# A recurrent stage rearranged: nine single instructions for the deviations, a mix 1024 columns wide, products and transposes in blocks

## The chip, the cores and the metric

One core of a Trainium2 chip runs the whole kernel. The metric is the time of one execution in microseconds (us); the median of three runs of the kernel before is 3341.35 us. The engines are PE (TensorE: matmuls, and transposes as matmuls with a unit matrix), PEld (its weight loads, which overlap with PE), DVE (VectorE), ACT (ScalarE), POOL (GpSimd) and SP (SyncE, which issues most DMAs). Each works through its own list of instructions in order. They meet at semaphores: counters that an instruction raises when it ends and that another engine's instruction waits for.

## The reference, cut to what matters

The program is a transformer over 128 graphs of 128 nodes with 128 channels, four stages that each add to x: graph attention, a mixture of experts, a second graph attention, and the recurrent stage. Only the last is changed:

```
x = x + _L0_gnn_ref(_layernorm(x), adj, ...)
x = x + _L0_ffn_ref(_layernorm(x), ...)
x = x + _L1_gnn_ref(_layernorm(x), adj, ...)
x = x + _L1_ffn_ref(_layernorm(x), ln_w, ln_b, W, b)

def step(h, _):                       # _L1_ffn_ref: 30 times
    h = h + 0.01 * jnp.tanh(h)
    h = h * jax.nn.sigmoid(h)
    h = _layernorm(h, ln_w, ln_b)     # (h - mu) * rsqrt(var + 1e-5) * w + bias, over the 128 channels
    h = jnp.einsum('bsc,dc->bsd', h, W) + b
    return (h, None)
```

All is float32.

## The kernel before, in words

`recurrent_ffn` (line 936 on) keeps all 128 x 128 rows of h on the chip, with the channels on the partitions and the rows (tokens) along the columns. They are cut into 16 chunks of 1024 columns (`g[:, c]`); a chunk is worked on in two units of 512 columns, u = 0 and 1. Chunk c in iteration i is called slot s = 16 i + c, and four chunks form a group. All engines walk through the slots in a written order (`body`), with the iterations 2 to 29 in a hardware loop (`Fori`).

One slot goes through these steps. The mean that the layer norm subtracts is folded into the weights beforehand (`w_centred`, line 1216), and the 1/sqrt(variance) is multiplied into g before the next product.

1. PE: the product of the weights with chunk c, per unit, into `p_y[:, s % 2]` in PSUM (`product`, line 1251). It waits until `g` has been scaled (`s_gs`) and, in `bank_taken`, until the mix of slot s-2 has read this half of the buffer.
2. ACT: `tanh`, from `p_y` to `th` (line 1305).
3. DVE: `mix`, th = 0.01 th + p_y (line 1130).
4. ACT: `silu` of the mix back into `g[:, c]` (line 1310); tanh and sigmoid work on the right side of the bias by the instruction's bias column.
5. PE: `transpose_g` (line 1263), four transposes of 128 columns per unit into `p_gt`. It waits for the silu, and for the statistics of the slot before on the same unit, since `p_gt` has one buffer.
6. DVE: `statistics` (line 1135), two BATCH_NORM_STATS2 instructions per unit, each over 256 columns of `p_gt`.

Once per group of four slots DVE turns 128 x 32 variances into deviations (`newton`, line 1143): variance plus epsilon, a seed by integer arithmetic on the float's bits, and three Newton steps of three instructions, 11 instructions in all (`CHAIN`). Each waits for the one before it (`s_nw`). `newton_part` (line 1165) puts two of them at each of two places in a slot, over three slots. Then PE transposes the deviations (`transpose_rstd`, line 1270), ACT copies them (line 1335), SP writes them to DRAM and reads them back spread over all partitions (`rb`, lines 1051 and 1056), and GpSimd multiplies g by them (`scale`, line 1069), in time for the next iteration. The last pass, `body(ITERS)`, has no mix; there `add_x` (line 1172) adds the last product to x and ACT issues the stores of the output.

The order of a slot before, per engine: DVE: mix of slot s-1 unit 1, statistics of s-2 unit 0, up to two of newton, mix of s unit 0, statistics of s-2 unit 1, up to two of newton. PE: product unit 0, transposes of s-2 unit 0, product unit 1, transposes of s-2 unit 1. ACT: tanh of s unit 0, silu of s-1 unit 1, (the copy), tanh of s unit 1, silu of s unit 0. Iteration 0 has transposes of the normalised x in place of the products, and ACT normalises x in it as well.

Of the kernel before, what the change touches and what calls it, by code (L numbers as in the profile page):

```python
# [20 lines left out]
P = 128  # L21
# [914 lines left out]
def recurrent_ffn(nc, env, x_sb, out_dram, ln_w, ln_b, w_dram, b_dram, N_TILES=128, ITERS=30):  # L936
# [11 lines left out]
    CHAIN, XCHAIN = 11, 12  # L948
    MAGIC = 1597463007.0
    OUTS = 4  # L950

    with ExitStack() as ctx:
# [20 lines left out]
        rstd = sb("rstd", [P, GTILES])  # L973
        rstd_row = sb("rstd_row", [GTILES, 2, P])
# [11 lines left out]
        v, work, v_x, work_x = (p_nw[:, n * GTILES:(n + 1) * GTILES] for n in range(4))  # L986
# [50 lines left out]
        with nc.Block() as block:  # L1037
# [52 lines left out]
            def _(dve):  # L1090
# [39 lines left out]
                def mix(s, b, u):  # L1130
                    dve.wait_ge(s_th, units(s, u))
                    nc.vector.scalar_tensor_tensor(out=th[:, b, cols(u)], in0=th[:, b, cols(u)], scalar=0.01,  # L1132
                                                   in1=p_y[:, b, cols(u)], op0=ALU.mult, op1=ALU.add).then_inc(s_u, 1)
# [9 lines left out]
                def newton(k, q, n):  # L1143

                    if n == 0:
# [3 lines left out]
                    else:  # L1149
                        dve.wait_ge(s_nw, CHAIN * k + n)  # L1150
                        if n == 1:
                            wait(dve, s_rt, k)
                            ins = nc.vector.tensor_scalar(rstd[:].bitcast(I32), v.bitcast(I32), -0.5, MAGIC,
                                                          ALU.mult, ALU.add)
                        elif n % 3 == 2:
                            ins = nc.vector.tensor_tensor(work, v, rstd[:], ALU.mult)  # L1156
                        elif n % 3 == 0:
                            ins = nc.vector.scalar_tensor_tensor(out=work, in0=work, scalar=-0.5, in1=rstd[:],  # L1158
                                                                 op0=ALU.mult, op1=ALU.mult)
                        else:  # L1160
                            ins = nc.vector.scalar_tensor_tensor(out=rstd[:], in0=work, scalar=1.5, in1=rstd[:],  # L1161
                                                                 op0=ALU.add, op1=ALU.mult)
                    ins.then_inc(s_nw, 1)

                def newton_part(i, c, place):

                    k, q = GROUPS * i + (c - 6) // GC, (c - 6) // GC % GROUPS
                    for n in range(4 * ((c - 6) % GC) + 2 * place, 4 * ((c - 6) % GC) + 2 * place + 2):
                        if n < CHAIN and live_group(k):
                            newton(k, q, n)  # L1170

                def add_x(o, u):
                    n = o * UNITS + u
                    dve.wait_ge(s_y, units(SLOTS + o, u))
                    wait(dve, s_out[n % OUTS], 16 * (n // OUTS))
# [40 lines left out]
                link(nc.vector.tensor_scalar(w_centred[:], w_centred[:], row_sum[:], float(np.sqrt(P)),  # L1216
# [10 lines left out]
                dve.wait_ge(s_xb, CHUNKS)  # L1227
                add_x(CHUNKS - 1, 1)

            @block.tensor  # L1230
            def _(pe):
# [6 lines left out]
                def bank_taken(s, u):  # L1238
# [3 lines left out]
                    else:  # L1242
                        wait(pe, s_u, units(s - 2, u))
# [31 lines left out]
                def body(i):  # L1275
                    for c in range(CHUNKS):
                        s = CHUNKS * i + c
                        for u in range(UNITS):
# [7 lines left out]
                            if live(s - 2):  # L1286
# [8 lines left out]
            def _(act):  # L1295
# [14 lines left out]
                def silu(s, c, u, col):  # L1310
                    act.wait_ge(s_u, units(s, u))
# [9 lines left out]
                def body(i):  # L1321
                    col = 0.0 if first(i) else bias[:]
                    for c in range(CHUNKS):
                        s = CHUNKS * i + c
                        if live(s):
                            tanh(s, c % 2, 0, col)
                        if live(s - 1):
                            silu(s - 1, (c - 1) % CHUNKS, 1, 0.0 if isinstance(i, int) and s - 1 < CHUNKS else bias[:])
# [7 lines left out]
                        if live(s):  # L1336
                            tanh(s, c % 2, 1, col)
# [77 lines left out]
```

## Time and profile before

| what | us |
|---|---|
| median of three runs (3338.03 to 3341.97) | 3341.35 |
| the profiled execution's own time | 3341.66 |
| its span, first to last instruction | 3339.9 |
| PE busy over the span | 3091.6 |
| DVE busy over the span | 2915.5 |
| ACT busy over the span | 2377.9 |
| POOL busy over the span | 1722.7 |

The recurrent stage is the last one: it starts at 1789 us with the statistics of x and lasts to the end of the span. Its iteration 0 runs up to about 1895 us, the 29 iterations with products of 512 columns up to about 3287, and the last pass with the stores to 3340. "Busy" is the sum of the instructions' durations with overlaps merged; an instruction's duration is longer than the distance from its start to the next one's start where the two overlap, so both are read: the duration from the groups, the distance from the times in the timeline. Where a row of the timeline merges several instructions (x2, x4), its second number goes from the first one's start to the last one's end.

### The profile page before, as it was taken

How to read it: one execution, taken by the hardware profiler on the slowest of the kernel's cores; microseconds unless marked ns; L12 is line 12 of the kernel's file. 1: busy time of each engine (PE TensorE's matmuls, PEld its weight loads, DVE VectorE, ACT ScalarE, POOL GpSimd, SP SyncE). 2: the span in 40 equal slices, each digit the busy share in tenths (PEclk: the TensorE clock that was granted, in tenths of full speed). 3: DMA queues.
4: the chain of work that ended last, by engine and by line, in shares of the span. 5: the costliest groups of instructions: out<-in, count | busy, mean ns of one | idle time of the engine just before them, and what ended most of it. 6: DMA issues, size and time to landing. Idle time of an engine off the chain costs nothing. (4 is left out here: it accounts for less than half of the span.)

```text
span 3339.9 us, 67477 instructions
## 1 busy us (share of the span) xinstructions
PE 3091.6 (93%) x16801; PEld 2062.9 (62%) x16801; DVE 2915.5 (87%) x8976; ACT 2377.9 (71%) x4988; POOL 1722.7 (52%) x1101
## 2 busy tenths in 40 slices
PE   7989986999998999999995799999999999999998
PEld 4666665888886777777774544444444444444446
DVE  5777776888887888888887799999999999999997
ACT  4666663444444777777776988888888888888883
POOL 2445444333332111121110388888888877777776
PEclk9999998999999999999996799999999999999999
DMA  4000000000000000000000255454555555454447
GB/s 129 16 16 16 19 13 14 1 0 0 0 0 17 14 13 9 13 13 13 9 6 3 81 182 176 174 174 176 177 177 177 177 177 177 177 177 176 172 173 239
DMA packets 135072, 290.04 MB, mean 87 GB/s; under 512 B 12081, under 2 KB 69601, under 8 KB 135009
## 3 DMA queue, kind: packets, MB, share of 16 engines
q1 hardware_dynamic: 118112, 280.89, 24.5%
q10 hardware_dynamic: 16896, 8.39, 0.9%
q8 instruction: 29, 0.48, 0.1%
q14 instruction: 35, 0.28, 0.0%
HBM read 278.88 MB, written 10.35 MB: 87 GB/s over the span
## 5 line engine op out<-in xcount | busy, mean ns | idle before, releaser
L1074 POOL TENSOR_TENSOR d_g<-d_g,d_rb 128x1024 f32<-128x1024 f32 x480 | 1120.6, 2369 | 380.6 <-DMA d_rb<-d_rstd_rows 380.2
L1253 PE MATMUL d_p_y<-d_g,d_w_main 128*128 128x512 f32 x1856 | 953.2, 595 | 0.1
L1267 PEld LDWEIGHTS d_p_gt<-ident,d_g 128*128 128x128 f32 x3840 | 436.6, 142 | 710.2 <-ACT d_g L1312 657.1
L1312 ACT ACTIVATE d_g<-d_th,d_bias 128x512 f32<-128x512 f32 x928 | 669.7, 722 | 182.1 <-DVE d_th L1132 174.7
L1139 DVE BATCH_NORM_STATS2 d_stats<-d_p_gt 128x6 f32<-128x256 f32 x1920 | 725.1, 419 | 23.1 <-PE d_p_gt L1267 23.0
L1132 DVE SCALAR_TENSOR_TENSOR d_th<-d_th,d_p_y 128x512 f32<-128x512 f32 x960 | 652.3, 680 | 14.2 <-ACT d_th L1308 7.9
L1267 PE MATMUL d_p_gt<-ident,d_g 128*128 128x128 f32 x3840 | 602.3, 280 | 64.9 <-ACT d_g L1312 23.1
L1308 ACT ACTIVATE d_th<-d_p_y,d_bias 128x512 f32<-128x512 f32 x928 | 622.0, 670 | 1.1 <-PE d_p_y L1253 1.0
L514 ACT ACTIVATE a_prob<-a_masked,a_neg_max 128x128 f32<-128x128 f32 x1024 | 327.4, 392 | 111.8 <-DVE a_neg_max L334 111.7
L434 PE MATMUL a_p_s<-a_k_heads,a_q_t 128*128 128x512 f32 x768 | 397.0, 599 | 0.6 <-DVE a_k_heads L310 0.6
L451 PEld LDWEIGHTS a_p_pv<-a_v_ones,a_prob_t 128*128 128x128 f32 x3072 | 375.1, 193 | 10.7 <-issue 10.3
L451 PE MATMUL a_p_pv<-a_v_ones,a_prob_t 128*128 128x17 f32 (+1 forms) x3072 | 376.7, 259 | 3.2 <-DVE a_context L347 2.0
L817 DVE SCALAR_TENSOR_TENSOR x_sb<-m_p_y,m_combine,x_sb 128x128 f32 (+1 forms) x1024 | 311.4, 343 | 68.1 <-PE m_p_y L859 55.2
L906 ACT ACTIVATE m_hidden<-m_p_h,m_cols 128x512 f32<-128x512 f32 x256 | 176.5, 689 | 225.9 <-PE m_p_h L851 225.9
L441 PEld LDWEIGHTS a_p_pt<-ident,a_prob 128*128 128x128 f32 x1536 | 192.4, 141 | 201.6 <-issue 198.5
L1253 PEld LDWEIGHTS d_p_y<-d_g,d_w_main 128*128 128x128 f32 x1856 | 280.4, 191 | 7.2 <-issue 5.7
L859 PEld LDWEIGHTS m_p_y<-m_w_sb,m_hidden 128*128 128x128 f32 x2048 | 266.0, 191 | 25.8 <-issue 3.5
L859 PE MATMUL m_p_y<-m_w_sb,m_hidden 128*128 128x128 f32 x2048 | 270.9, 275 | 0.0
L321 DVE TENSOR_TENSOR a_masked<-a_p_s,a_mask 128x512 f32<-128x512 f32 x256 | 176.1, 688 | 83.7 <-PE a_p_s L434 82.6
L248 POOL TENSOR_TENSOR x_sb<-x_sb,a_out_bias 128x512 f32 (+1 forms) x32 | 42.1, 1316 | 385.7 <-DVE a_masked L321 339.3
L527 ACT COPY a_prob_t<-a_p_pt 128x512 f32<-128x512 f32 x384 | 221.7, 577 | 17.0 <-PE a_p_pt L441 17.0
L230 POOL TENSOR_TENSOR a_rstd<-a_var,minus_half 128x4 f32<-128x4 f32 x64 | 66.3, 1037 | 323.0 <-DVE a_var L292 323.0
(167 smaller groups left out, 4443.7 us busy)
## 6 DMA issues: line engine op xcount, KB each, us to landing
d_rb<-d_rstd_rows SPq DMA_DIRECT2D x480, 512.0 KB, 5.5
a_adj_in<-in_adj_dram SPq DMA_DIRECT2D x64, 256.0 KB, 2.8
out_dram<-d_out_sb ACTq DMA_DIRECT2D x32, 256.0 KB, 3.2
d_rstd_rows<-d_rstd_row SPq DMA_DIRECT2D x120, 16.0 KB, 1.4
m_w_sb<-in_L_ffn_w_dram SPq DMA_DIRECT2D x2, 512.0 KB
x_sb<-in_x_dram SPq DMA_DIRECT2D x1, 256.0 KB, 2.9
a_w_raw<-in_L_gnn_Wq_dram SPq DMA_DIRECT2D x2, 64.0 KB, 2.2
a_w_raw<-in_L_gnn_Wk_dram SPq DMA_DIRECT2D x2, 64.0 KB, 2.1
```

What stands on the lines that cost most here:

```text
L434: nc.tensor.matmul(p_s[:, u % 2], q_t[:, par, g * P:(g + 1) * P], k_heads[:, par, g, h0:h0 + HU, :], start=mask_on_vector, stop=True).then ...
L451: last = nc.tensor.matmul(p_pv[:, h, :], prob_t[:, u % 2, h, :], v_ones[:, par, g, h0 + h, :], start=True, stop=True)
L514: last = nc.scalar.activation(prob[:, u % 2, h, :], scores_src[:, u % 2, h, :], ACT.Exp, bias=neg_max[:, u % 2, h:h + 1], scale=EXP_SCALE)
L817: last = nc.vector.scalar_tensor_tensor(out=x_tile, in0=p_y[:, e % 2, t, :], scalar=combine[:, par, t, e:e + 1], in1=x_tile, op0=ALU.mult, ...
L859: last = nc.tensor.matmul(p_y[:, e % 2, t, :], hidden[:, e % 2, t * P:(t + 1) * P], w2_sb[:, e, :], start=True, stop=True)
L1074: nc.gpsimd.tensor_tensor(g[:, c, :], g[:, c, :], rb[:, buf, :], ALU.mult).then_inc(s_gs, 1)
L1132: nc.vector.scalar_tensor_tensor(out=th[:, b, cols(u)], in0=th[:, b, cols(u)], scalar=0.01, in1=p_y[:, b, cols(u)], op0=ALU.mult, op1=ALU. ...
L1139: ins = nc.vector.bn_stats(stats[:, q % 2, (j * CT + t) // 2].rearrange("p a s -> p (a s)"), p_gt[:, t * P:(t + 2) * P].rearrange("p (a c) ...
L1253: nc.tensor.matmul(p_y[:, c % 2, cols(u)], w_main[:], g[:, c, cols(u)], start=True, stop=True).then_inc(s_y, 1)
L1267: ins = nc.tensor.transpose(p_gt[:, t * P:(t + 1) * P], g[:, c, t * P:(t + 1) * P], ident[:])
L1308: nc.scalar.activation(th[:, b, cols(u)], p_y[:, b, cols(u)], ACT.Tanh, bias=col).then_inc(s_th, 1)
L1312: nc.scalar.activation(g[:, c, cols(u)], th[:, c % 2, cols(u)], ACT.Silu, bias=col).then_inc(s_g, 1)
```

## The change: what it does

- The deviations take nine instructions in place of eleven: variance plus epsilon, the seed, one cubic step (n = 2 to 5) and one square step (n = 6 to 8). The cubic step leaves out a factor of 3/8, which goes into the weights once (`RSTD_SCALE`) and into the constant of n = 7. The work tile `newton_work` is in SBUF, no longer in PSUM.
- They stand one at a time at three places of a slot, in three of four slots.
- `mix` is one instruction over the 1024 columns of a slot; it waits for both tanh and raises `s_u` once. `silu` and `bank_taken` wait for the whole mix.
- DVE's order in a slot is: statistics of s-2 unit 0, newton, mix of s, newton, statistics of s-2 unit 1, newton. In the last pass both sums of a chunk stand at the place of the mix.
- PE's order is: both products, then both blocks of transposes (then, once per group, the deviations).
- ACT's order is: (the copy), both tanh of s, both silu of s-1.

```diff
-    CHAIN, XCHAIN = 11, 12
+    CHAIN, XCHAIN, PLACES = 9, 12, 3
+    RSTD_SCALE = 3.0 / 8.0
+        newton_work = sb("newton_work", [P, GTILES])
...
-                def mix(s, b, u):
-                    dve.wait_ge(s_th, units(s, u))
-                    nc.vector.scalar_tensor_tensor(out=th[:, b, cols(u)], in0=th[:, b, cols(u)], scalar=0.01,
-                                                   in1=p_y[:, b, cols(u)], op0=ALU.mult, op1=ALU.add).then_inc(s_u, 1)
+                def mix(s, b):
+                    dve.wait_ge(s_th, units(s, UNITS - 1))
+                    nc.vector.scalar_tensor_tensor(out=th[:, b], in0=th[:, b], scalar=0.01, in1=p_y[:, b],
+                                                   op0=ALU.mult, op1=ALU.add).then_inc(s_u, 1)
...
+                        elif n == 2 or n == 6:
+                            ins = nc.vector.tensor_tensor(work, v, y, ALU.mult)
+                        elif n == 3:
+                            ins = nc.vector.tensor_tensor(work, work, y, ALU.mult)
+                        elif n == 4:
+                            ins = nc.vector.scalar_tensor_tensor(out=work, in0=work, scalar=-10.0 / 3.0, in1=work,
+                                                                 op0=ALU.add, op1=ALU.mult)
+                        elif n == 7:
+                            ins = nc.vector.scalar_tensor_tensor(out=work, in0=work, scalar=-0.5 * RSTD_SCALE ** 2, in1=y,
+                                                                 op0=ALU.mult, op1=ALU.mult)
+                        else:
+                            ins = nc.vector.scalar_tensor_tensor(out=y, in0=work, scalar=5.0 if n == 5 else 1.5, in1=y,
+                                                                 op0=ALU.add, op1=ALU.mult)
...
-                    for n in range(4 * ((c - 6) % GC) + 2 * place, 4 * ((c - 6) % GC) + 2 * place + 2):
-                        if n < CHAIN and live_group(k):
-                            newton(k, q, n)
+                    n = PLACES * ((c - 6) % GC) + place
+                    if n < CHAIN and live_group(k):
+                        newton(k, q, n)
...
                         s = CHUNKS * i + c
-                        if live(s - 1):
-                            mix(s - 1, (c - 1) % 2, 1)
-                        elif last(i):
-                            add_x(c - 1, 1)
                         if live(s - 2):
                             statistics(s - 2, (c - 2) % CHUNKS, 0)
                         newton_part(i, c, 0)
                         if live(s):
-                            mix(s, c % 2, 0)
+                            mix(s, c % 2)
                         else:
                             add_x(c, 0)
+                            add_x(c, 1)
+                        newton_part(i, c, 1)
                         if live(s - 2):
                             statistics(s - 2, (c - 2) % CHUNKS, 1)
-                        newton_part(i, c, 1)
+                        newton_part(i, c, 2)
...
-                        wait(pe, s_u, units(s - 2, u))
+                        wait(pe, s_u, s - 1)
...
                                 product(s, c, u)
-                            if live(s - 2):
+                        if live(s - 2):
+                            for u in range(UNITS):
                                 transpose_g(s - 2, (c - 2) % CHUNKS, u)
...
-                    act.wait_ge(s_u, units(s, u))
+                    act.wait_ge(s_u, s + 1)
...
-                        if live(s):
-                            tanh(s, c % 2, 1, col)
-                            silu(s, c, 0, col)
+                        for u in range(UNITS):
+                            if live(s):
+                                tanh(s, c % 2, u, col)
+                        for u in range(UNITS):
+                            if live(s - 1):
+                                silu(s - 1, (c - 1) % CHUNKS, u, 0.0 if isinstance(i, int) and s - 1 < CHUNKS else bias[:])
```

## Rows read from the trace of the kernel before

**Rows 1.** The page's first part: busy us, share of the span, instructions.
```profile
PE 3091.6 (93%) x16801; PEld 2062.9 (62%) x16801; DVE 2915.5 (87%) x8976; ACT 2377.9 (71%) x4988; POOL 1722.7 (52%) x1101
```

**Rows 2.** Stretches: length, busy us of PE, PEld, DVE, ACT, POOL, granted clock, DMA, GB/s.
```profile
1830.00:1870.00 40.00, 23.68 (x114) 20.41 (x115) 30.38 (x97) 37.55 (x88) 0.00 (x0) 0.64 0.06 14
...
2000.00:2500.00 500.00, 476.40 (x2037) 241.94 (x2037) 489.25 (x1458) 434.48 (x707) 410.02 (x176) 1.00 0.51 177
```

**Rows 3.** Groups from 2000 to 3280 us: busy us, mean ns, idle before and releaser.
```profile
L1139 DVE BATCH_NORM_STATS2 d_stats<-d_p_gt 128x6 f32<-128x256 f32 x1703 | 643.0, 419 | 0.0
...
L1132 DVE SCALAR_TENSOR_TENSOR d_th<-d_th,d_p_y 128x512 f32<-128x512 f32 x852 | 579.2, 680 | 9.2 <-issue 5.1 <-ACT d_th L1308 3.2
L1308 ACT ACTIVATE d_th<-d_p_y,d_bias 128x512 f32<-128x512 f32 x852 | 571.0, 670 | 0.0
```

**Rows 4.** Waits from 2000 to 3280 us: us in total, times, longest.
```profile
PEld d_p_gt L1267 <- ACT d_g L1312: 608.6, 800, 1.4
POOL d_g L1074 <- DMA d_rb<-d_rstd_rows: 255.0, 101, 3.8
ACT d_g L1312 <- DVE d_th L1132: 161.1, 534, 0.7
```

**Rows 5.** Timeline, the transpose of the deviations (start us, us, instruction).
```profile
2500.21 0.27 PE L1273 MATMUL d_p_row<-ident,d_rstd 128*32 128x128 f32 x1
...
2524.52 0.27 PE L1273 MATMUL d_p_row<-ident,d_rstd 128*32 128x128 f32 x1
...
2548.32 0.27 PE L1273 MATMUL d_p_row<-ident,d_rstd 128*32 128x128 f32 x1
```

**Rows 6.** Timeline: DVE with one instruction of the deviations and without; one product.
```profile
2510.85 0.76 DVE L1139 BATCH_NORM_STATS2 d_stats<-d_p_gt 128x6 f32<-128x256 f32 x2
...
2511.52 0.17 DVE L1161 SCALAR_TENSOR_TENSOR d_rstd<-d_p_nw,d_rstd 128x32 f32<-128x32 f32 x1
...
2511.61 0.68 DVE L1132 SCALAR_TENSOR_TENSOR d_th<-d_th,d_p_y 128x512 f32<-128x512 f32 x1
...
2512.21 0.76 DVE L1139 BATCH_NORM_STATS2 d_stats<-d_p_gt 128x6 f32<-128x256 f32 x2
...
2512.33 1.02 PE L1253 MATMUL d_p_y<-d_g,d_w_main 128*128 128x512 f32 x2
2512.88 0.67 DVE L1132 SCALAR_TENSOR_TENSOR d_th<-d_th,d_p_y 128x512 f32<-128x512 f32 x1
...
2513.47 0.75 DVE L1139 BATCH_NORM_STATS2 d_stats<-d_p_gt 128x6 f32<-128x256 f32 x2
```

**Rows 7.** Groups by shape before 1800 us: the two-input DVE instruction of 1024 columns.
```profile
L741 DVE TENSOR_TENSOR m_w_lo<-m_w_sb,m_w_hi 128x1024 fp32r<-128x1024 f32 x1 | 1.2, 1226 | 0.0
```

**Rows 8.** The chain of waits from 2500 to 2506 us: start us, us, what.
```profile
2500.37 0.11 PE d_p_row L1273
2500.48 0.86 PE d_p_y L1253 x2
...
2502.64 0.44 PE d_p_gt L1267 x4
```

**Rows 9.** Timeline: hand-overs from PE to DVE and from DVE to PE.
```profile
1846.28 1.06 PE L1267 MATMUL d_p_gt<-ident,d_g 128*128 128x128 f32 x4
...
1847.38 0.76 DVE L1139 BATCH_NORM_STATS2 d_stats<-d_p_gt 128x6 f32<-128x256 f32 x2 [1.35 <-PE d_p_gt L1267]
...
2517.84 1.12 PE L1253 MATMUL d_p_y<-d_g,d_w_main 128*128 128x512 f32 x2
2517.94 0.76 DVE L1139 BATCH_NORM_STATS2 d_stats<-d_p_gt 128x6 f32<-128x256 f32 x2
...
2518.75 0.42 PEld L1267 LDWEIGHTS d_p_gt<-ident,d_g 128*128 128x128 f32 x4 [0.61 <-DVE d_stats L1139]
2518.80 0.60 PE L1267 MATMUL d_p_gt<-ident,d_g 128*128 128x128 f32 x4
```

**Rows 10.** Timeline of the last pass: one sum and what it waited for.
```profile
3306.46 0.69 DVE L1177 TENSOR_TENSOR d_out_sb<-d_p_y,x_sb 128x512 f32<-128x512 f32 x1 [3.75 <-DMA out_dram<-d_out_sb]
```

More of the change, by code:

```diff
@@ L985, in recurrent_ffn @@
         p_rt = p_row[0:GTILES, 0:P]
-        v, work, v_x, work_x = (p_nw[:, n * GTILES:(n + 1) * GTILES] for n in range(4))
+        v, v_x, work_x = (p_nw[:, n * GTILES:(n + 1) * GTILES] for n in range(3))
         s_load = sem("weights_loaded")
@@ L1143, in newton @@
                 def newton(k, q, n):
+                    y, work = rstd[:], newton_work[:]
                     if n == 0:
@@ L1152, in newton @@
                             wait(dve, s_rt, k)
[L1153 to L1158, printed above, removed]
+                            ins = nc.vector.tensor_scalar(y.bitcast(I32), v.bitcast(I32), -0.5, MAGIC, ALU.mult, ALU.add)
+                        elif n == 2 or n == 6:
[7 more added lines that the diff above has]
+                            ins = nc.vector.scalar_tensor_tensor(out=work, in0=work, scalar=-0.5 * RSTD_SCALE ** 2, in1=y,
                                                                  op0=ALU.mult, op1=ALU.mult)
                         else:
-                            ins = nc.vector.scalar_tensor_tensor(out=rstd[:], in0=work, scalar=1.5, in1=rstd[:],
+                            ins = nc.vector.scalar_tensor_tensor(out=y, in0=work, scalar=5.0 if n == 5 else 1.5, in1=y,
                                                                  op0=ALU.add, op1=ALU.mult)
@@ L1174, in add_x @@
                     dve.wait_ge(s_y, units(SLOTS + o, u))
+                    dve.wait_ge(s_xb, CHUNKS)
                     wait(dve, s_out[n % OUTS], 16 * (n // OUTS))
@@ L1215, in _ @@
                 link(nc.vector.tensor_scalar(row_sum[:], row_sum[:], 1.0 / P, None, ALU.mult))
-                link(nc.vector.tensor_scalar(w_centred[:], w_centred[:], row_sum[:], float(np.sqrt(P)),
+                link(nc.vector.tensor_scalar(w_centred[:], w_centred[:], row_sum[:], RSTD_SCALE * float(np.sqrt(P)),
                                              ALU.subtract, ALU.mult))
@@ L1226, in _ @@
                 iterations(dve, body)
-                dve.wait_ge(s_xb, CHUNKS)
-                add_x(CHUNKS - 1, 1)
             @block.tensor
@@ L1324, in body @@
                         s = CHUNKS * i + c
-                        if live(s):
-                            tanh(s, c % 2, 0, col)
-                        if live(s - 1):
-                            silu(s - 1, (c - 1) % CHUNKS, 1, 0.0 if isinstance(i, int) and s - 1 < CHUNKS else bias[:])
                         k, q = GROUPS * i + (c - 10) // GC, (c - 10) // GC % GROUPS
@@ L1335, in body @@
                             nc.scalar.copy(rstd_row[:, q % 2, :], p_rt).then_inc(s_row, 1)
-                        if live(s):
-                            tanh(s, c % 2, 1, col)
-                            silu(s, c, 0, col)
+                        for u in range(UNITS):
[4 more added lines that the diff above has]
+                                silu(s - 1, (c - 1) % CHUNKS, u, 0.0 if isinstance(i, int) and s - 1 < CHUNKS else bias[:])
                         if first(i) and c + 1 < CHUNKS:
```

## The prediction

> **What bounds the kernel now.** I read four views in this order. The page's first part [rows 1] has TensorE (PE) 93% and VectorE (DVE) 87% busy over the whole span, which doesn't say which of them sets the time here. The table of stretches [rows 2] does more: from 2000 to 2500 us, inside the recurrent stage, PE is busy 476 us of 500, DVE 489 and ScalarE (ACT) 434, at full granted clock. The groups of that stage and its waits [rows 3, 4] say who is late. DVE's two large groups have next to no idle time before them, while ACT's silu stood 161 us for DVE's mix, and the transposes' weight loads stood 609 us for that silu. DVE sets the pace, and ACT and PE follow.
>
> The pace is read off the transpose of the deviations, one per group of four slots [rows 5]. Two groups with the loop's end in them take 24.31 us, the two without it 23.80. One iteration (16 slots) is 48.11 us, 3.01 a slot; the loop's end costs 0.51, and a quiet group is 11.90. DVE's starts [rows 6] account for it: half a slot without deviations is 0.67 (two statistics) + 0.59 (mix) = 1.26 us, eight of them 10.08, and the other 1.82 us are the eleven instructions of the deviations. In pairs they are dear, since the second waits for the first one's result. The one that stands alone lets the mix start 0.09 after it.
>
> **The change on DVE.** Removed per group: eleven small instructions, 1.82 us. Added: nine that stand alone. The row of the single one gives 0.09; at most each costs its whole 0.17 [rows 6]. I take 0.10, near the only row of a single one: 0.90 us. Eight mixes of 512 columns at 0.59 become four of 1024. The stage has no such row. The nearest is a two-input instruction of 1024 columns in another stage, 1226 ns [rows 7], against 680 for the 512-wide mix [rows 3]: 0.546 more for 512 more columns. From the start of a wide mix to the next start that makes 0.59 + 0.546, taken as 1.13. Bounds: 1.09 if no part of it is fixed (twice 0.546), 1.18 if nothing is saved. DVE's own work in a group is then 8 x 0.67 + 4 x 1.13 + 0.90 = 10.78 us, 2.70 a slot, against 11.90 for the group now.
>
> A rule that speaks against this: the row shows an instruction of 0.17 us, and the next starts 0.09 us after it [rows 6]. The Trainium skill (VectorE: DVE Perf Modes, The DRAIN you can't avoid) says that the next one does not start before the pipe is empty. By it half a slot would now be 2 x 0.42 + 0.68 = 1.52 us [rows 3] instead of the 1.26 read, so the trace disagrees.
>
> **The others' own work.** PE per slot: two product blocks of 0.86, two transpose blocks of 0.44, and the transpose of the deviations, 0.11 per group [rows 8]: 2.63 us. ACT: 434/500 of 3.01 is 2.61, its overlaps counted twice. GpSimd: 410 us over 176 instructions [rows 2] is 2.33. None exceeds 2.70. GpSimd stood 255 us for the spread rows [rows 4]; a shorter period takes from this idle time, of which a group of 11.43 us still leaves 2.1, and the deviations come no later. I cost it at nothing; with that cover gone GpSimd would need 2.33 a slot, still less than DVE.
>
> **What the blocks add: a round through PE and DVE.** The transposes of unit 1 overwrite columns that the statistics of the slot before must have read. Those statistics (unit 1) now stand behind the wide mix on DVE. Behind the waiting transposes stand, in PE's queue, both products of the next slot and then its transposes of unit 0; for these DVE's next statistics wait, and a mix behind them. One turn covers two slots. From the start of mix s:
> - wide mix 1.13, a small one 0.10, the two statistics of unit 1 to their end 0.76 [rows 9]: 1.99
> - the weight load 0.05 later, the first transpose 0.05 after it [rows 9], the block 0.44 [rows 8]: 2.53
> - two product blocks, 2 x 0.86: 4.25
> - the transposes of unit 0, first start to last end, 0.60, and 0.04 to DVE [rows 9]: 4.89
> - two statistics 0.67, a small one 0.10, and mix s+2 starts: 5.66 us.
>
> The way through the tanh is shorter: from the second product's start 1.02 + 0.67 and two hand-overs of 0.04 are 1.77 [rows 3, 6], against 0.86 + 0.60 + 0.04 + 0.67 + 0.10 = 2.27. The round costs 2.83 us a slot where DVE alone could do 2.70, so it sets the pace. A group holds two turns and the transpose of the deviations: 11.43. An iteration is 4 x 11.43 + 0.51 = 46.23 us, 1.88 less than 48.11. The stage runs 29 such iterations: 54.5 us.
>
> The Trainium skill (Perfetto Trace Analysis, Optimizing Scalar/DVE Operations) puts both sides: larger operations help a saturated engine, smaller ones may be better where the engine leaves bubbles on others. It gives some 125 ns as the fixed cost of a DVE operation on PSUM; no row here shows that much. By that figure the merged mix would save some 0.07 us more per slot, an estimate of 16 us over the stage with the round in force.
>
> **The ends.** Iteration 0 is set by ACT (37.6 us busy of 40 [rows 2]). Its list of work is the same there, only silu and tanh change places: 0, within 5 us either way. In the last pass the sums wait for the stores of the output (3.75 us before one of them [rows 10]), and those don't change. The last deviations now stand behind one more such sum, but the copy on ACT that takes them already stood behind that sum's store: +0.5 us, at most one such wait of 3.75.
>
> **Sum.** The profiled execution took 3341.66 us (span 3339.9 and 1.8 around it). 3341.7 - 54.5 + 0.5 = 3288 us. The median of the runs, 3341.35, is 0.3 lower, which changes nothing.
>
> **Rivals.**
> - *DVE alone sets the pace.* The round would have to close in less than 5.3 us. A group is then 10.78, an iteration 43.63, the gain 29 x 4.48 = 130 us: 3212. For it: every engine has less than 2.70 of its own, and DVE is the bound today. Against: each hop of the round has its row, and none is 0.3 too long.
> - *Behind a wait nothing overlaps: slower.* Place: the same round, which breaks even at (48.11 - 0.51 - 0.44)/8 = 5.89 us, only 0.23 above my sum. A product block that starts fresh reads 1.12 [rows 9] instead of 1.02 [rows 6]: +0.10. Two small instructions at their whole 0.17: +0.14. The mix at 1.18: +0.05. That is 5.95, an iteration of 48.55, +13 us: 3354. Against: behind a real wait for statistics [rows 9] the transposes show 0.60 as elsewhere.
> - *By the rule of the empty pipe: slower.* Each DVE instruction at its whole duration: statistics 0.84 instead of 0.76 and 0.67, mix 1.226 (1.13), two small ones 0.17 (0.10) make the round 6.15 and the iteration 50.1: 3401. The rows of today refute it, 1 in 100. It is the rule of the Trainium skill weighed above (VectorE: DVE Perf Modes, The DRAIN you can't avoid).
> - *The hand-overs eat all: no change.* The round between 5.86 and 5.92, 3341. Same evidence as for the second, in a narrow band.
>
> That the deviations don't get cheaper as told is unlikely: each of the nine has two statistics or a mix before it in the order written out.
>
> **Chances.** The round near 5.66 (5.55 to 5.80, 3262 to 3320): 0.62. DVE alone, or between both (3205 to 3262): 0.16. A small gain (3320 to 3334): 0.04. No change: 0.07. Slower: 0.11, 0.01 of it by the empty pipe. A measurement of this kernel can't tell less than 0.2% (6.7 us) from no change. So faster 0.82, same 0.07, slower 0.11. The range, 3210 to 3330, takes in DVE alone and leaves out most of no change and slower; the likeliest case's own is 3262 to 3320.
>
> **What would show it.** DVE: mixes of 1024 columns at about 1.22 us, small instructions never in pairs. The transposes of the deviations 11.4 us apart in a quiet group (10.8: DVE alone; 11.9: no gain). PE idle about 0.2 us before the transposes of unit 1, put down to the statistics, and DVE idle about 0.1 us before the statistics of unit 0, put down to the transposes. The silu no longer waits for the mix. I am wrong if DVE waits for the tanh instead, if no engine waits for the transposes, or if the granted clock leaves 1.00 in the stage.

## The result, and the profile after

The kernel after takes 3861.48 us (median of 4 runs, 3854.85 to 3867.11), the kernel before 3340.03 (4 runs, 3338.03 to 3341.97). The ratio is 1.1561, with a 95% interval of 1.154 to 1.1581: it became slower by 16%, 521 us. Forecast were 3288 us, faster, and at most 3330.

The first part of the page after stands beside [rows 1]:

```profile
PE 3195.3 (83%) x16801; PEld 2163.1 (56%) x16801; DVE 3341.2 (87%) x8256; ACT 2401.3 (62%) x4988; POOL 1717.9 (45%) x1101
```

DVE issues 720 instructions fewer and is busy for 426 us more. So some of its instructions became longer. The second stretch of [rows 2] (length, busy us of PE, PEld, DVE, ACT, POOL, granted clock, DMA, GB/s):

```profile
2000.00:2500.00 500.00, 376.94 (x1495) 204.05 (x1494) 474.16 (x887) 324.64 (x519) 299.54 (x129) 0.94 0.35 127
```

In 500 us PE issues 1495 instructions where it issued 2037. The instruction counts of ACT and GpSimd fall by the same 27%. DVE alone stays near full, at 474 us with 887 instructions. DVE's groups by shape, from 2000 to 3700 us, answer to [rows 3] (busy us, mean ns of one, idle before and releaser):

```profile
L1142 DVE BATCH_NORM_STATS2 d_stats<-d_p_gt 128x6 f32<-128x256 f32 x1664 | 624.3, 415 | 99.0 <-PE d_p_gt L1272 99.0
L1135 DVE SCALAR_TENSOR_TENSOR d_th<-d_th,d_p_y 128x1024 f32<-128x1024 f32 x416 | 501.0, 1204 | 0.0
L1169 DVE SCALAR_TENSOR_TENSOR d_rstd<-d_newton_work,d_rstd 128x32 f32<-128x32 f32 x208 | 303.6, 1460 | 0.0
L1163 DVE SCALAR_TENSOR_TENSOR d_newton_work<-d_newton_work 128x32 f32<-128x32 f32 x104 | 148.6, 1429 | 0.0
L1161 DVE TENSOR_TENSOR d_newton_work<-d_newton_work,d_rstd 128x32 f32<-128x32 f32 x104 | 61.0, 586 | 0.0
L1166 DVE SCALAR_TENSOR_TENSOR d_newton_work<-d_newton_work,d_rstd 128x32 f32<-128x32 f32 x104 | 51.9, 499 | 0.0
L1159 DVE TENSOR_TENSOR d_newton_work<-d_p_nw,d_rstd 128x32 f32<-128x32 f32 x208 | 35.1, 169 | 0.0
L1151 DVE TENSOR_SCALAR d_p_nw<-d_stats 128x32 f32<-128x32 f32 x104 | 19.4, 186 | 0.0
L1157 DVE TENSOR_SCALAR d_rstd<-d_p_nw 128x32 int32<-128x32 int32 x104 | 18.9, 182 | 0.0
```

Statistics and mixes are as long as expected. Of the deviations' instructions, all on tiles of 128x32, three lines take 169 to 186 ns and four take 499 to 1460. What sets the two kinds apart is in the operand names: the slow lines read two tiles in SBUF (`newton_work` and `rstd`, or `newton_work` twice), L1159 reads one in PSUM (`p_nw`) and one in SBUF, L1151 and L1157 have one tensor input. Five instructions of a group's nine are of the slow kind (L1169 is two of them).

DVE in time, from 2503 to 2508.5 us (start us, us, instruction), beside [rows 6]:

```profile
2503.73 1.72 DVE L1163 SCALAR_TENSOR_TENSOR d_newton_work<-d_newton_work 128x32 f32<-128x32 f32 x1
2505.38 0.75 DVE L1142 BATCH_NORM_STATS2 d_stats<-d_p_gt 128x6 f32<-128x256 f32 x2
2506.05 1.71 DVE L1169 SCALAR_TENSOR_TENSOR d_rstd<-d_newton_work,d_rstd 128x32 f32<-128x32 f32 x1
2507.68 0.75 DVE L1142 BATCH_NORM_STATS2 d_stats<-d_p_gt 128x6 f32<-128x256 f32 x2
2508.35 0.17 DVE L1159 TENSOR_TENSOR d_newton_work<-d_p_nw,d_rstd 128x32 f32<-128x32 f32 x1
```

And GpSimd beside it, from three windows:

```profile
2503.04 2.37 POOL L1077 TENSOR_TENSOR d_g<-d_g,d_rb 128x1024 f32<-128x1024 f32 x1 [7.76 <-DMA d_rb<-d_rstd_rows]
...
2505.34 4.69 POOL L1077 TENSOR_TENSOR d_g<-d_g,d_rb 128x1024 f32<-128x1024 f32 x2
...
2507.65 4.68 POOL L1077 TENSOR_TENSOR d_g<-d_g,d_rb 128x1024 f32<-128x1024 f32 x2
```

A product of GpSimd runs from 2503.04 to 2505.41, the next from 2505.34, the one after from 2507.65. DVE's slow instructions end at 2505.45 and 2507.76: each 0.04 to 0.05 us after a product of GpSimd has ended. The first began 0.69 us after its product did, and lasted for what was left of it. Between 2000 and 3100 us all 67 of L1163 and 112 of 134 of L1169 have the end of a GpSimd instruction inside them. The Trainium skill (SBUF — State Buffer, Who interferes with whom) has this as a rule: a DVE instruction with two SBUF inputs takes its second input through a read interface that it shares with GpSimd, and contends there with a GpSimd instruction that reads SBUF. The Trainium skill (SBUF — State Buffer, SBUF: two separate sides) calls the shared pair an exclusive lock: the one that starts first has it for the whole instruction, and the other is blocked. The trace agrees, with 1.43 and 1.46 us in place of 0.17.

The waits of 2000 to 3700 us answer to [rows 4] (us in total, times, longest):

```profile
POOL d_g L1077 <- DMA d_rb<-d_rstd_rows: 698.6, 104, 11.0
ACT d_th L1314 <- PE d_p_y L1258: 400.6, 667, 3.5
PEld d_p_gt L1272 <- ACT d_g L1318: 348.4, 274, 3.8
PE d_p_gt L1272 <- DVE d_stats L1142: 337.6, 289, 3.6
```

DVE's lag is handed round: PE stands up to 3.6 us for the statistics, ACT up to 3.5 for the products, GpSimd up to 11 for the rows that the late deviations give. The transposes of the deviations stand much further apart than in [rows 5]:

```profile
2496.61 0.27 PE L1278 MATMUL d_p_row<-ident,d_rstd 128*32 128x128 f32 x1
2512.44 0.28 PE L1278 MATMUL d_p_row<-ident,d_rstd 128*32 128x128 f32 x1 [0.91 <-DVE d_rstd L1169]
2530.35 0.39 PE L1278 MATMUL d_p_row<-ident,d_rstd 128*32 128x128 f32 x1 [0.92 <-DVE d_rstd L1169]
```

A group takes 15.83 and 17.91 us here. From the first of these transposes to the last (120 in both kernels, 119 distances) it is 1962.1 us after and 1446.6 before, 515.4 us more, where the whole span of the profiled executions grew by 513.3. Before the first and behind the last nothing is lost (-1.0 and -1.2). All of it is in the 119 groups, 4.33 us each.

### The profile page after: what moved, and what is told of

Same layout as the page of the kernel before. It is cut to its first block, busy times and chain, and to the rows that moved or that the text cites. A ratio compares the mean times of both kernels' runs of the same rounds, so it can differ in the third digit from the quotient of the medians.

```text
span 3853.1 us, 66901 instructions
## 1 busy us (share of the span) xinstructions
PE 3195.3 (83%) x16801; PEld 2163.1 (56%) x16801; DVE 3341.2 (87%) x8256; ACT 2401.3 (62%) x4988; POOL 1717.9 (45%) x1101
## 4 chain that ended last, share of the span: by engine, by line
DVE 25%; issue 13%; PE 12%; ACT 2%; DVEq 1%; DMA 1%; ACTq 0%
PE d_p_y L1258 8%; DVE d_stats L1142 8%; DVE d_rstd L1169 7%; DVE d_newton_work L1163 4%; PE d_p_gt L1272 3%; DVE d_newton_work L1161 2%; DVE d_newton_work L1166 1%; ACT d_g L1307 1%; DVE d_th L1135 1%; PE d_p_row L1278 1%; DVE d_newton_work L1159 1%; DMA out_dram<-d_out_sb 1%; DVE d_p_nw L1151 1%; DVE d_rstd L1157 1%; DVEq L1154 0%
## 5 line engine op out<-in xcount | busy, mean ns | idle before, releaser
L1258 PE MATMUL d_p_y<-d_g,d_w_main 128*128 128x512 f32 x1856 | 965.3, 646 | 0.1
L1314 ACT ACTIVATE d_th<-d_p_y,d_bias 128x512 f32<-128x512 f32 x928 | 637.0, 686 | 460.2 <-PE d_p_y L1258 452.2
L1272 PEld LDWEIGHTS d_p_gt<-ident,d_g 128*128 128x128 f32 x3840 | 464.9, 148 | 773.9 <-ACT d_g L1318 392.8
L1318 ACT ACTIVATE d_g<-d_th,d_bias 128x512 f32<-128x512 f32 x928 | 614.7, 711 | 45.3 <-DVE d_th L1135 45.2
L1135 DVE SCALAR_TENSOR_TENSOR d_th<-d_th,d_p_y 128x1024 f32<-128x1024 f32 x480 | 578.1, 1204 | 3.8 <-ACT d_th L1314 3.8
L1258 PEld LDWEIGHTS d_p_y<-d_g,d_w_main 128*128 128x128 f32 x1856 | 340.1, 204 | 260.8 <-issue 254.7
L1169 DVE SCALAR_TENSOR_TENSOR d_rstd<-d_newton_work,d_rstd 128x32 f32<-128x32 f32 x240 | 343.5, 1431 | 0.1
L441 PE MATMUL a_p_pt<-ident,a_prob 128*128 128x128 f32 x1536 | 230.5, 273 | 0.3 <-ACT a_prob_t L527 0.3
```

The costliest lines, as they stand in the source:

```text
L441: last = nc.tensor.transpose(p_pt[:, h, :], prob[:, b, h, :], ident[:])
L1135: nc.vector.scalar_tensor_tensor(out=th[:, b], in0=th[:, b], scalar=0.01, in1=p_y[:, b], op0=ALU.mult, op1=ALU.add).then_inc(s_u, 1)
L1169: ins = nc.vector.scalar_tensor_tensor(out=y, in0=work, scalar=5.0 if n == 5 else 1.5, in1=y, op0=ALU.add, op1=ALU.mult)
L1258: nc.tensor.matmul(p_y[:, c % 2, cols(u)], w_main[:], g[:, c, cols(u)], start=True, stop=True).then_inc(s_y, 1)
L1272: ins = nc.tensor.transpose(p_gt[:, t * P:(t + 1) * P], g[:, c, t * P:(t + 1) * P], ident[:])
L1314: nc.scalar.activation(th[:, b, cols(u)], p_y[:, b, cols(u)], ACT.Tanh, bias=col).then_inc(s_th, 1)
```

## The experiments

Three theories stood at the start. **A:** two inputs in SBUF make a DVE instruction wait for GpSimd's running product, and nothing else is wrong. **B:** the blocks and the wide mix are at fault, and the long small instructions only show it (for e2: a small instruction doesn't care where its work tile lies). **C:** A is right, and the round through PE and DVE is longer than predicted too. Medians, with the ratio to the kernel before on the same chip (e4 and e9 leave out most of GpSimd's work and show waits only, not a usable kernel):

| kernel | us | ratio (95%) | iteration, us |
|---|---|---|---|
| e1: after, work in PSUM, ten instructions | 3351.23 | 1.0038 (1.0024 to 1.0052) | 48.39 |
| e2: before, work in SBUF | 3675.53 | 1.0995 (1.0963 to 1.1026) | |
| e3: after, GpSimd's product in quarters | 3482.50 | 1.0443 (1.0423 to 1.0463) | |
| e4: after, GpSimd scales 8 columns | 3311.12 (one run) | | 46.44, some 48.1 |
| e8: after, only the square reads two SBUF inputs | 3469.47 | 1.04 (1.0362 to 1.0438) | |
| e9: after, GpSimd almost only writes | 3297.10 (one run) | | |
| e5: e1, deviations transposed later | 3298.24 | 0.9873 (0.9857 to 0.9889) | 46.45 |
| e6: e5, statistics ahead of the mix | 3217.39 | 0.9628 (0.9612 to 0.9644) | 43.69 |
| e7: before, ten single instructions | 3240.48 | 0.9703 (0.9687 to 0.9719) | 44.69 |

**e1: the work tile back in PSUM.** Every kernel here keeps to at most one PSUM tile among an instruction's inputs, and the square needs the same tile twice. So the square is written as a product with a second tile, `newton_side`, in SBUF, and the cubic step takes one instruction more.

```diff
-    CHAIN, XCHAIN, PLACES = 9, 12, 3
+    CHAIN, XCHAIN, PLACES = 10, 12, 3
-        v, v_x, work_x = (p_nw[:, n * GTILES:(n + 1) * GTILES] for n in range(3))
+        v, v_x, work_x, newton_work = (p_nw[:, n * GTILES:(n + 1) * GTILES] for n in range(4))
...
-    (n == 4)  out=work, in0=work, scalar=-10.0 / 3.0, in1=work, op0=ALU.add, op1=ALU.mult
+    (n == 4)  out=side, in0=work, scalar=-10.0 / 3.0, in1=y, op0=ALU.add, op1=ALU.mult
+    (n == 5)  tensor_tensor(work, work, side, ALU.mult)
+    (n == 6)  out=y, in0=y, scalar=5.0, in1=work, op0=ALU.mult, op1=ALU.add
```

> The changed kernel with the work tile of the deviations back in PSUM, so that no DVE instruction of the deviations reads two SBUF tiles; since a square of a PSUM tile can't be written as one instruction, the cubic step takes one more (ten instructions in all, the tenth alone in the fourth slot). Theory A (a DVE instruction with two SBUF inputs waits until GpSimd's running instruction ends): each small instruction lasts 0.17 to 0.20 us again, the group comes down from 16.3 us to the 11.4 us of the prediction's round, and the time is 3265 to 3320 us. Theory B (the wide mix and the blocks are at fault, the long small instructions only show it): the time stays above 3700 us. Theory C (A is right, and the round through PE and DVE is longer than predicted): small instructions short, 3330 to 3450 us.

Measured: 3351.23 us. DVE's groups from 2000 to 3200 us:

```profile
L1159 DVE TENSOR_TENSOR d_p_nw<-d_p_nw,d_rstd 128x32 f32<-128x32 f32 x198 | 36.7, 186 | 0.0
...
L1163 DVE SCALAR_TENSOR_TENSOR d_newton_side<-d_p_nw,d_rstd 128x32 f32<-128x32 f32 x99 | 17.8, 180 | 0.0
...
L1166 DVE TENSOR_TENSOR d_p_nw<-d_p_nw,d_newton_side 128x32 f32<-128x32 f32 x99 | 17.6, 178 | 0.0
L1174 DVE SCALAR_TENSOR_TENSOR d_rstd<-d_p_nw,d_rstd 128x32 f32<-128x32 f32 x100 | 17.1, 171 | 0.0
```

All ten are at 0.17 to 0.19 us in the mean, those that write SBUF (L1163, L1174) too. They meet GpSimd as often as ever: from 2000 to 3100 us 648 of 909 start while one of its instructions runs, and none of them lasts more than 0.20 us. B falls, and of the three forecasts C's is the one met (3330 to 3450; A's was 3265 to 3320). 510 of the 521 us are gone. The granted clock of 2000 to 2500 us was 0.94 in the kernel after (58 us at the lower of its two levels, 1.2 GHz, the rest at 2.4 GHz) and is 1.00 here, with the same matmuls and without PE's long stalls. What is left, 13 us over before on the same chip, is in the order of work. In time:

```profile
2500.89 1.21 DVE L1135 SCALAR_TENSOR_TENSOR d_th<-d_th,d_p_y 128x1024 f32<-128x1024 f32 x1
...
2503.64 1.21 DVE L1135 SCALAR_TENSOR_TENSOR d_th<-d_th,d_p_y 128x1024 f32<-128x1024 f32 x1
...
2506.60 1.21 DVE L1135 SCALAR_TENSOR_TENSOR d_th<-d_th,d_p_y 128x1024 f32<-128x1024 f32 x1
...
2509.26 0.17 DVE L1174 SCALAR_TENSOR_TENSOR d_rstd<-d_p_nw,d_rstd 128x32 f32<-128x32 f32 x1
2509.35 1.21 DVE L1135 SCALAR_TENSOR_TENSOR d_th<-d_th,d_p_y 128x1024 f32<-128x1024 f32 x1
2509.49 0.28 PE L1283 MATMUL d_p_row<-ident,d_rstd 128*32 128x128 f32 x1
...
2512.89 1.21 DVE L1135 SCALAR_TENSOR_TENSOR d_th<-d_th,d_p_y 128x1024 f32<-128x1024 f32 x1
```

Two slots take 5.71 us (2500.89 to 2506.60, 2503.64 to 2509.35), but 6.29 (2506.60 to 2512.89) where the tenth instruction (2509.26) lies between: PE's transpose of the deviations (2509.49) stands ahead of the products of the next slot and waited for it. That gave e5.

**e2: the kernel before, with only the work tile in SBUF.**

```diff
+        newton_work = sb("newton_work", [P, GTILES])
-        v, work, v_x, work_x = (p_nw[:, n * GTILES:(n + 1) * GTILES] for n in range(4))
+        v, v_x, work_x = (p_nw[:, n * GTILES:(n + 1) * GTILES] for n in range(3))
+        work = newton_work[:]
```

> The kernel before with one edit alone: the work tile of the deviations in SBUF instead of PSUM. Six of its eleven instructions per group then read two SBUF tiles. Theory A: in the changed kernel five such instructions cost a group about 4.9 us, about 1 us each; six make about 5.5 us, the group goes from 12.0 to about 17.5 us and the time to 3850 to 4100 us. Theory B: no change, 3325 to 3355 us.

Measured: 3675.53 us, slower than before by 10% without any other part of the change. Its groups from 2000 to 3200 us:

```profile
L1160 DVE SCALAR_TENSOR_TENSOR d_newton_work<-d_newton_work,d_rstd 128x32 f32<-128x32 f32 x240 | 183.0, 762 | 5.5
L1163 DVE SCALAR_TENSOR_TENSOR d_rstd<-d_newton_work,d_rstd 128x32 f32<-128x32 f32 x239 | 144.2, 603 | 2.7
L1158 DVE TENSOR_TENSOR d_newton_work<-d_p_nw,d_rstd 128x32 f32<-128x32 f32 x240 | 42.8, 178 | 2.7
```

The same split, and B, which forecast no change, is refuted here too. A's size was missed (3850 to 4100 us): I counted nearly every such instruction as held, but by their starts and ends only some 40% are, 94 of 219 of L1160 and 86 of 219 of L1163 from 2000 to 3100 us. The trace says which. Of these 438 instructions 182 start while a GpSimd instruction runs, and 180 of them are held (the other two start within 1 ns of its start). The other 256 start with GpSimd idle, and none is held. The two of the last Newton step are held in 178 of 179 cases (1950 to 3300 us), since GpSimd's products of the group run then; the four of the first two steps mostly fall into GpSimd's wait for the spread rows.

**e3: GpSimd's product in four instructions of 256 columns.** If A holds, an instruction waits for a quarter, not for the whole.

```diff
-                    nc.gpsimd.tensor_tensor(g[:, c, :], g[:, c, :], rb[:, buf, :], ALU.mult).then_inc(s_gs, 1)
+                    for part in range(4):
+                        pc = slice(part * 256, (part + 1) * 256)
+                        ins = nc.gpsimd.tensor_tensor(g[:, c, pc], g[:, c, pc], rb[:, buf, pc], ALU.mult)
+                    ins.then_inc(s_gs, 1)
```

> The changed kernel with each GpSimd product of 1024 columns cut into four of 256 columns. Theory A: the blocked DVE instruction gets in when a quarter ends, so its mean falls from 1.4 to 1.7 us to at most 0.7 us, and the time falls to 3300 to 3450 us. Theory A2 (blocked until GpSimd has no instruction ready at all): no shorter, 3800 us or more. Theory B: the small instructions don't depend on GpSimd's lengths, 3800 to 3900 us.

Measured: 3482.5 us, above the 3300 to 3450 that A gave. Groups from 2000 to 3100 us:

```profile
L1079 POOL TENSOR_TENSOR d_g<-d_g,d_rb 128x256 f32<-128x256 f32 x1319 | 913.2, 737 | 156.1 <-DMA d_rb<-d_rstd_rows 156.1
...
L1164 DVE TENSOR_TENSOR d_newton_work<-d_newton_work,d_rstd 128x32 f32<-128x32 f32 x82 | 103.9, 1267 | 0.0
L1172 DVE SCALAR_TENSOR_TENSOR d_rstd<-d_newton_work,d_rstd 128x32 f32<-128x32 f32 x166 | 74.1, 446 | 0.0
L1166 DVE SCALAR_TENSOR_TENSOR d_newton_work<-d_newton_work 128x32 f32<-128x32 f32 x82 | 32.6, 398 | 0.0
```

Three of the four slow lines are as expected: they fell with the length of GpSimd's instruction, from 1460 and 1429 ns to 446 and 398. The fourth, L1164, rose from 586 to 1267. It has seven very long ones among 120, and this is one:

```profile
2322.98 13.29 DVE L1164 TENSOR_TENSOR d_newton_work<-d_newton_work,d_rstd 128x32 f32<-128x32 f32 x1
```

18 quarters of GpSimd ended while it lasted, and it ended only when their run did (then GpSimd stood for 14.6 us). By A as I had it, it should have come in behind the first; the seven behave as the expectation's A2 has it. Without these seven, 92 us together, the time would be about 3390, an estimate, within what was expected.

**e4 and e9: GpSimd does next to nothing, or only writes.** Both leave out the scaling of all but 8 columns of each chunk.

```diff
-                    nc.gpsimd.tensor_tensor(g[:, c, :], g[:, c, :], rb[:, buf, :], ALU.mult).then_inc(s_gs, 1)
+  e4:               nc.gpsimd.tensor_tensor(g[:, c, 0:8], g[:, c, 0:8], rb[:, buf, 0:8], ALU.mult).then_inc(s_gs, 1)
+  e9:               nc.gpsimd.tensor_tensor(g[:, c, 0:8], g[:, c, 0:8], rb[:, buf, 0:8], ALU.mult)
+                    nc.gpsimd.memset(rb[:, buf, 8:], 1.0).then_inc(s_gs, 1)
```

> The changed kernel with GpSimd multiplying only 8 of the 1024 columns of a chunk (the scaling of the rest is left out, waits and order as they are). Theory A: every small DVE instruction lasts about 0.17 to 0.20 us, and the time is that of the round, 3265 to 3320 us. Theory C: short instructions, 3330 to 3450 us. Theory B: 3700 us or more.

> The changed kernel with GpSimd's product cut to 8 columns, as in e4_scale_8_columns, and behind it a memset of the other 1016 columns of the spread buffer: GpSimd is busy for about 1 us per chunk, but writes SBUF without reading it (the scaling is left out). If what the DVE instructions with two SBUF inputs wait for is GpSimd's reading: small instructions 0.17 to 0.20 us, group 11.55 us, 3290 to 3325 us, as e4_scale_8_columns (3311). If any GpSimd access to SBUF blocks them: they last until the memset ends, up to 1 us, and the time is 3350 us or more.

Measured: 3311.12 and 3297.1 us. In e9, from 2000 to 3000 us:

```profile
L1078 POOL MEMSET d_rb<- 128x1016 f32 x344 | 325.5, 946 | 0.0
...
L1167 DVE SCALAR_TENSOR_TENSOR d_newton_work<-d_newton_work,d_rstd 128x32 f32<-128x32 f32 x86 | 15.7, 183 | 0.0
L1164 DVE SCALAR_TENSOR_TENSOR d_newton_work<-d_newton_work 128x32 f32<-128x32 f32 x86 | 15.5, 180 | 0.0
```

With the code of DVE unchanged from after, the nine instructions are short in both, but for a few in e4. A memset of 946 ns per slot, which reads nothing, holds none of them up: of the 431 with two SBUF inputs from 2000 to 3000 us, 256 start while one runs, and the longest of these is 0.18 us. It is GpSimd's reading that holds them. In e4 nine of the 240 of L1169 still wait for GpSimd's preparation of x (2.37 us each), in the first 16 iterations, where an iteration is up to 48.3 us; without these it is 46.44.

**e8: as after, but only the square reads two SBUF inputs** (the price of keeping nine instructions).

```diff
-    (n == 3)  tensor_tensor(work, work, y, ALU.mult)
+    (n == 3)  tensor_tensor(side, work, y, ALU.mult)         # work in PSUM, side in SBUF
-    (n == 4)  out=work, in0=work, scalar=-10.0 / 3.0, in1=work
+    (n == 4)  out=work, in0=side, scalar=-10.0 / 3.0, in1=side
```

> The changed kernel with nine instructions of which only one, the square of the cubic step, reads two SBUF tiles; the other eight have their work tile in PSUM. Theory A: one blocked instruction per group of 1.2 to 1.4 us on average in place of five, all others 0.17 to 0.20 us; with no stall the group would be 11.55 us, so it is 12.4 to 12.9 us and the time 3370 to 3450 us. Were the cost the SBUF work tile as such and not the count of blocked instructions, it would stay near 3850 us.

Measured: 3469.47 us. From 2000 to 3000 us:

```profile
L1163 DVE SCALAR_TENSOR_TENSOR d_p_nw<-d_newton_side 128x32 f32<-128x32 f32 x78 | 126.5, 1621 | 0.0
L1159 DVE TENSOR_TENSOR d_p_nw<-d_p_nw,d_rstd 128x32 f32<-128x32 f32 x155 | 27.9, 180 | 0.0
```

One such instruction in nine makes the kernel 4% slower than before, while its eight neighbours stay short. That is 19 us above A's range of 3370 to 3450: the instruction lasts 1.62 us, where 1.2 to 1.4 was expected. It always comes at the same place of the group, where GpSimd is at work, so most are held: 66 of 85 from 2000 to 3100 us.

**e5: e1 with the transpose of the deviations later in PE's list** (behind the products of its next slot; ACT's copy behind both tanh).

```diff
+                                product(s, c, u)
+                        k = GROUPS * i + (c - 10) // GC
+                        if c % GC == 2 and live_group(k):
+                            transpose_rstd(k)
                         if live(s - 2):
-                        k = GROUPS * i + (c - 9) // GC
-                        if c % GC == 1 and live_group(k):
-                            transpose_rstd(k)
```

> The ten instructions in PSUM as in e1_ten_psum, and PE's transpose of the deviations one slot later, behind the products of the fourth slot's successor, with ACT's copy behind both tanh. In e1_ten_psum PE stood about 0.4 us per group for the tenth instruction and the group took 12.02 us; with nine and a near-idle GpSimd it took 11.55. If that wait explains the 0.47 us between them: group 11.5 to 11.6 us, 3285 to 3315 us. If ten instructions are dear in themselves: 12.0 us and 3340 to 3355 us.

Measured: 3298.24 us, 0.9873 of before. The iteration is 46.45 us (forecast: 46.23). DVE from 2503 us on:

```profile
2503.72 0.76 DVE L1142 BATCH_NORM_STATS2 d_stats<-d_p_gt 128x6 f32<-128x256 f32 x2 [0.33 <-PE d_p_gt L1277]
...
2504.49 1.22 DVE L1135 SCALAR_TENSOR_TENSOR d_th<-d_th,d_p_y 128x1024 f32<-128x1024 f32 x1
...
2509.55 0.76 DVE L1142 BATCH_NORM_STATS2 d_stats<-d_p_gt 128x6 f32<-128x256 f32 x2 [0.43 <-PE d_p_gt L1277]
...
2510.33 1.21 DVE L1135 SCALAR_TENSOR_TENSOR d_th<-d_th,d_p_y 128x1024 f32<-128x1024 f32 x1
```

From mix to mix two slots on, 2504.49 to 2510.33, with DVE idle at the end of the turn, for the transposes of unit 0: this is the round of the prediction, 5.84 us with the transpose of the deviations (0.11) in it.

**e6: e5 with both blocks of statistics ahead of the wide mix.** If the round is what limits, taking the mix out of it (1.13 us) leaves DVE's own work as the limit.

```diff
                         newton_part(i, c, 0)
+                        if live(s - 2):
+                            statistics(s - 2, (c - 2) % CHUNKS, 1)
+                        newton_part(i, c, 1)
                         if live(s):
                             mix(s, c % 2)
...
-                        newton_part(i, c, 1)
-                        if live(s - 2):
-                            statistics(s - 2, (c - 2) % CHUNKS, 1)
                         newton_part(i, c, 2)
```

> As e5_rstd_later, with both units' statistics ahead of the wide mix on DVE, so that the transposes of unit 1 no longer wait for statistics that stand behind the mix. If the round through PE and DVE sets the 11.55 us group, it is gone and DVE's own work (8 x 0.67 + 4 x 1.13 + 10 x 0.10 = 10.9 us) sets the pace: an iteration of about 44.1 us, 3210 to 3260 us. If the pace is set by something else in the blocks (ACT's order, PE's weight loads): 3285 to 3350 us as e5_rstd_later.

Measured: 3217.39 us, 0.9628 of before and the fastest of all. The stretch from 2000 to 2500 us, of e5 first and then of e6:

```profile
2000.00:2500.00 500.00, 475.40 (x2112) 274.34 (x2111) 474.31 (x1293) 446.94 (x734) 427.12 (x184) 1.00 0.52 182
```

```profile
2000.00:2500.00 500.00, 500.00 (x2247) 297.32 (x2246) 498.56 (x1373) 474.34 (x779) 453.47 (x196) 1.00 0.56 194
```

DVE goes from 474 to 499 us, an iteration from 46.45 to 43.69. PE is shown as full too, but its ends are modelled; neither its wait for the statistics (3.8 us of weight loads from 2000 to 3000 us are left of it) nor DVE's for the transposes is there any more. The same instructions in another order: 81 us.

**e7: the kernel before with the ten single instructions alone** (work in PSUM, order and mixes as before).

> The kernel before with one part of the change alone: the deviations by ten single instructions (work tile in PSUM, one SBUF input at most), at three places of a slot; mixes of 512 columns and the old order stay. DVE's sum per group is 8 x 1.26 + 10 x 0.10 = 11.1 us instead of 11.9. If DVE alone bounds that order: 3250 to 3285 us. If the old order has a round of its own near 11.9: 3320 to 3345 us.

Measured: 3240.48 us, 0.9703 of before, 10 us below the range of DVE alone (3250 to 3285). The ten small instructions alone are worth 100 us; adding blocks and wide mix as the change orders them, with the later transpose of the deviations (e5), gives 58 of these back; with the statistics ahead as well (e6) they add 23.

## Why the prediction was wrong

**The step that failed** is the second of "The change on DVE": "Added: nine that stand alone. The row of the single one gives 0.09; at most each costs its whole 0.17 [rows 6]. I take 0.10". Five of the nine are not instructions of that row. It reads `d_rstd<-d_p_nw,d_rstd`, one tile in PSUM and one in SBUF, and the change moves `newton_work` to SBUF, so that both are there. The move stood in the diff, and I told it in the list of edits and priced it at nothing. With it fails the sentence that GpSimd costs nothing: only its own lateness was weighed, not what it keeps from others, though [rows 2] has it at work 410 us of 500. The right memories alone would not have given the price. The kernel before has two-input instructions of this shape on SBUF tiles in its mixture-of-experts stage, 32 of this one, and none starts while a GpSimd instruction runs:

```profile
L764 DVE SCALAR_TENSOR_TENSOR m_others<-m_first,m_logits 128x32 f32<-128x32 f32 x32 | 5.8, 182 | 0.0
```

An estimate from above was in the rows: GpSimd's product is 410/176 = 2.33 us, and an instruction that waits for one can take that long.

The sum with the measured sizes: L1169 twice 1.29 us over its 0.17, L1163 1.26, L1161 0.42, L1166 0.33 make 4.59 us per group. With 11.56 for the mean forecast group (46.23/4, the loop's end included) that is 16.15, where 1700 us / 104 groups = 16.35 are measured. e1 (these inputs in PSUM), e9 (GpSimd doesn't read) and e2 (the move alone) each show it from another side.

Point by point:

- *DVE is the bound before, small instructions in pairs are dear:* right. e7 changes only them: an iteration falls from 48.11 to 44.69, 0.86 us a group. The forecast takes 1.82 away and adds nine at 0.10; for ten it gives 0.82. That agrees by luck in part: a quiet group falls by 0.75 only (11.90 to 11.15), the rest is the loop's end, which costs 0.1 us in place of 0.51.
- *The mix of 1024 columns, 1.13 from start to start:* right. 2507.24 to 2508.37 in e5.
- *The round, 5.66 us for two slots:* the mechanism was right, and nearly its size, though the kernel after hides it. It is 5.71 in e1, between mixes with no deviations to transpose. The quiet group of e5 is 11.55 or 11.56 (forecast 11.43), and e6, which opens the round, gains 81 us. PE waits for the statistics and DVE for the transposes, as told, each longer than told (0.29 us in the mean against 0.2, and 0.41 against 0.1, though DVE's in only 107 turns of 172). The waits of e5 from 2000 to 3000 us (in total, times, longest):

```profile
PE d_p_gt L1277 <- DVE d_stats L1142: 49.4, 172, 0.4
DVE d_stats L1142 <- PE d_p_gt L1277: 43.9, 107, 0.4
```

- *PE's transpose of the deviations costs 0.11:* wrong with ten instructions (e1: 0.58 more in its turn), because it must wait for the last of them; right where it stands later. With nine, in e4, it is no wait: 11.55.
- *The sum, 3288:* e5 is the nearest to the kernel that was forecast, with the inputs in PSUM, a tenth instruction for that, and the transpose moved out of its way. It takes 3298, inside the likeliest case's range. By the starts of the products in the two traces, the 29 iterations gave 46.0 us instead of 54.5, iteration 0 cost 3.0 (0 within 5), the tail 0.5 (+0.5). An iteration is 46.45 for 46.23 because two errors offset each other: the four groups are 0.5 us longer than told, and the loop's end, carried over unchanged as 0.51, costs about 0.24.
- *DVE alone, 43.63 an iteration, 3212:* this rival is nearest to e6, 43.69 and 3217. It needed another order, and that the figures are so close is luck in part: a group there is 10.94 for 10.78, and the loop's end costs nothing for 0.51.
- *The empty pipe:* refuted again, mixes start 0.09 after a small instruction of 0.17. The prediction quoted the rule without its limit: the Trainium skill (VectorE: DVE Perf Modes, The DRAIN you can't avoid) goes on that a next instruction that is not held starts earlier.
- *"I am wrong if ... the granted clock leaves 1.00":* it did, 0.94. It isn't the cause of the stalls: e1 changes only DVE's small instructions, and with the stalls gone the clock is back at 1.00 with the same matmuls.
- The range and the rivals held no case in which an instruction of DVE gets longer. "Slower" had 0.11, all of it for the round, at 3354 to 3401: the right sign for a wrong reason.

Not settled: how much of the 0.20 us a group between 16.15 and 16.35 is the lower clock, and which of the stalls sets a group's end.

## What to carry to other kernels

A tile that changes its memory changes the instructions that read it: take the price of each from a row with the same operands in the same memories and with the same engines at work beside it (L764 has the memories and not the company), and if there is none, reckon with the longest instruction of the engine that shares the way to it. Even that isn't a firm bound where short ones follow each other without a gap (e3, 12.6 us and more). An instruction's mean in a group tells little where it can wait inside itself, since no wait is recorded: compare groups of one shape, and look what ends at the moment when the long one does. And ask of a merged instruction what now stands behind it: the same mix and statistics in another order were worth 81 us.

## What the runs showed of the hardware

- A DVE instruction whose two tensor inputs are both in SBUF is held while GpSimd runs a product of 1024 columns that reads SBUF, up to its whole 2.37 us, and ends 0.04 to 0.06 us after it. It is so in 180 of the 182 cases of e2 in which it starts during one, and in none of the 256 in which it doesn't. With one of the inputs in PSUM it never is (at most 0.20 us in e1), nor beside a GpSimd memset of 0.95 us (e9). The hold is inside the recorded duration; the trace names no wait.
- Not every GpSimd instruction with SBUF inputs holds it for its recorded length. In the kernel before all 32 of L772 (two SBUF inputs, 128x32) start during a GpSimd instruction of 128x4 that is recorded for 1.01 us, and last 0.18 to 0.19 us. How the hold depends on the columns read wasn't tried between 8 (e9, where at most 0.22 us was seen) and 256 (e3).
- With short GpSimd instructions back to back (0.74 us), a TENSOR_TENSOR of this kind lasted through 17 to 19 of their ends, 12.6 to 14.0 us (7 of 120 in e3). The SCALAR_TENSOR_TENSOR ones were not (at most 1.27 us). Why the two differ wasn't tried.
- The granted clock was 0.94 (58 of 500 us at 1.2 GHz, the rest at 2.4) in the stage where PE stood up to 3.6 us at a time, and 1.00 where it waited for the statistics or the silu for 0.4 us at most (e5).
